# A transformer block on one core: rotations, masks, scalings and blanking of slots moved between VectorE, ScalarE and GpSimd, loads issued earlier, two layer norms folded into one

## The reference, cut to what matters

```python
# layer 0 attention: no weights; rotary turn of q = norm(x) and k = ctx, causal, 16 heads of 8
q, k = rope(heads(norm(x))), rope(heads(ctx)); out = softmax(mask(q k^T / sqrt(8))) v,  v = heads(ctx)
# layer 0 "ffn": a graph of 6 nodes, each an attention of 8 heads of 16 on weighted edges
q = ew[c,0]*(nodes[a] @ We + be); k, v likewise; nodes[c] = act_w[c]*(mha(q,k,v) @ Wo) + q
out = norm(nodes[5], 1e-6)*ln_g + ln_b
# layer 1 attention: its input is normed once by the block and once by the layer
xn = norm(norm(x))*gamma + beta; q = xn @ w_q; k, v = split(ctx @ w_kv); 16 heads of 64
# layer 1 ffn: 8-bit fake quantisation.  layer 2 attention: q = norm(x), k = v = ctx, causal and padded
# layer 2 ffn: quantised.  layer 3 attention: four projections.  layer 3 ffn: top-2 of 32 experts
```

## Time and profile before

| | us |
|---|---|
| median of 3 runs | 1889.33 (1886.15 to 1894.91) |
| the profiled execution's own time | 1894.12 |
| its span | 1892.3 |
| PE busy | 1303.1 (69%) |
| DVE busy | 1224.2 (65%) |
| ACT busy | 836.7 (44%) |
| POOL busy | 476.5 (25%) |

### The profile page before, as it was taken

The page is one execution under the profiler, slowest core; times in us unless marked ns, Lnnn a source line. Parts: engine busy times, 40 slices in busy tenths (PEclk is TensorE's granted clock), DMA queues, the critical chain, the costliest instruction groups (busy, mean ns, idle before and its releaser), DMA issues. The chain is left out here.

```text
span 1892.3 us, 32152 instructions
## 1 busy us (share of the span) xinstructions
PE 1303.1 (69%) x12243; PEld 922.7 (49%) x12245; DVE 1224.2 (65%) x2458; ACT 836.7 (44%) x1294; POOL 476.5 (25%) x650
## 2 busy tenths in 40 slices
PE   0798179999999991499899882179833688530674
PEld 0465056666666660366666650146622455320674
DVE  5665337777777777666776756836657577558444
ACT  1255226676776771355555532225513156410330
POOL 6343232222222201222222222134310200000452
PEclk9999579999999996599999996579965789965787
DMA  2243312222222222000000000122101122143434
GB/s 72 51 65 43 99 59 85 86 88 86 91 85 86 90 65 68 1 1 1 1 1 1 1 1 11 28 52 54 37 12 32 35 52 53 46 153 87 158 123 124
DMA packets 115782, 108.20 MB, mean 57 GB/s; under 512 B 44766, under 2 KB 99230, under 8 KB 114590
## 3 DMA queue, kind: packets, MB, share of 16 engines
q1 hardware_dynamic: 113582, 103.49, 19.8%
q0 software_dynamic: 2048, 2.65, 0.6%
HBM read 44.00 MB, written 8.71 MB: 28 GB/s over the span
## 5 line engine op out<-in xcount | busy, mean ns | idle before, releaser
L595 ACT ACTIVATE Pt<-bank 128x1024 f32<-128x1024 f32 (+1 forms) x384 | 366.4, 954 | 176.3 <-PE bank L539 174.7
L651 DVE TENSOR_REDUCE l0f_Mf<-bank 128x4 f32<-128x1024 f32 x192 | 234.5, 1221 | 108.8 <-PE bank L518 108.8
L559 PE MATMUL bank<-Pt,V 128*32 128x256 f32 (+1 forms) x3072 | 196.9, 375 | 10.7 <-POOL Pt L400 9.5
L1127 POOL TENSOR_TENSOR Psum<-Pt 128x512 f32<-128x512 f32 x64 | 83.5, 1305 | 269.8 <-ACT Pt L1259 269.8
L400 POOL TENSOR_SCALAR_AFFINE_SELECT Pt<-Pt 128x512 f32<-128x512 f32 x128 | 81.9, 640 | 176.1 <-ACT Pt L595 176.1
L559 PEld LDWEIGHTS bank<-Pt,V 128*32 128x32 f32 x3072 | 81.5, 111 | 82.3 <-issue 26.2
L416 POOL CAST parts<-nodes 128x256 fp32r<-128x256 f32 x96 | 38.4, 400 | 306.5 <-PE bank L490 306.5
L539 PE MATMUL bank<-l0f_QK 64*128 64x256 f32 x768 | 97.6, 333 | 19.4 <-DMA l0f_QK<-l0f_NMrow 18.9
L841 PE MATMUL bank<-ident,Qf 128*128 128x128 f32 x64 | 14.4, 418 | 140.2 <-SPq L243 91.6
L1297 DVE TENSOR_TENSOR qk_lo<-bank,qk_hi 128x512 fp32r<-128x512 f32 x64 | 44.2, 690 | 99.3 <-ACT qk_hi L1251 99.3
L651 DVE TENSOR_REDUCE l2x_Mf<-bank 128x4 f32<-128x1024 f32 x64 | 76.9, 1221 | 32.3 <-PE bank L518 32.2
(11 more groups left out here) (397 smaller groups left out, 3363.0 us busy)
## 6 DMA issues: line engine op xcount, KB each, us to landing
l0f_QK<-l0f_Z SPq DMA_DIRECT2D x288, 128.0 KB, 2.3
l2x_QK<-l2x_Z SPq DMA_DIRECT2D x96, 128.0 KB
V<-in_L_experts SPq DMA_DIRECT2D x8, 960.0 KB
Wg<-in_L_experts SPq DMA_DIRECT2D x8, 960.0 KB, 12.1
l0x_QK<-l0x_Z SPq DMA_DIRECT2D x48, 128.0 KB
tokB<-s_cand SPq DMA_DIRECT2D x16, 200.0 KB
s_y_even<-in_c_zero SPq DMA_DIRECT2D x1, 2048.0 KB, 11.2
s_y_odd<-in_c_zero SPq DMA_DIRECT2D x1, 2048.0 KB, 16.1
```

What stands on the lines that cost most here:

```text
L559: last = pe.matmul(bank[4][32 * x:32 * x + 32, o + q0:o + S], Va[:, 2 * n + k, 4 * j + x, :], Pp[:, (f + x // 2) % 4, x % 2, k * S:k * S + ...
L595: act.activation(Pp[:, g % 4, :, 0:w], banks[:, 2:4, 0:w], ACT.Exp, scale=L.scale).then_inc(exp_done, 1)
L651: d.tensor_reduce(m, A.rearrange("p h (t k) -> p h t k", t=2), AX, ALU.max).then_inc(max_done, 1)
L1127: e.tensor_tensor(Psum[:, q % 2], Pp[:, q % 4, :, 0:S], Pp[:, q % 4, :, S:2 * S], ALU.add).then_inc(key_sum, 1)
```

## The change

1. The loads of the first attention (`tA`, `ctxS`, `rope`, `rowk`) go to the head of `setup_sp`; `X` goes behind the barrier into `l0x_sp`. `setup_sp` then awaits nine loads. `rowk` is loaded once and its three later loads are gone. POOL clears `V` and writes the ones before the first barrier.
2. The rotation of `ctx` goes from POOL to DVE, in two halves, each put behind a request for a mean to PE.
3. Both halves of all slots are written by ACT (`slots_blank`), part of them before the root of the norm, part behind it: 6 of 128x2048, in the graph 8 of 128x1024. `queries_blank` and `keys_blank` are gone.
4. The graph's 12 scalings of weights go from POOL to DVE. After the graph the gate is multiplied in with `ln_g`, and POOL, behind its part of the flow, adds the gated `ln_b` to `X`; DVE has one instruction less over the whole of `X`.
5. Layer 1's loads (`l1x_in_sp`) and high parts (`l1x_in_act`) are issued before the barrier `l0f_end`. Its two norms become one, with the variance times 1.00001 plus 1e-10. POOL makes three low parts before the next barrier and the others, in pieces, behind it; PE waits for the pieces by `w_lo`. `Esel` is made from an 8-column sum and one copy.
6. Before layer 2 the values' copy goes from POOL to ACT and the mask to DVE.
7. Three semaphores of the expert part (`m_token`, `xg_out`, and the count) are replaced by `dma_out`.

The diff, without the plain renamings:

```diff
         y_full, y_done = sem("y_full"), sem("y_done")
         wd_in, w_full, w_hi, w_done = sem("wd_in"), sem("w_full"), sem("w_hi"), sem("w_done")
 
-        def queries_blank(g, L):
-
-            for r in range(L.ring):
-                g.eng.tensor_copy(L.QK[:, r, :, 0, :], bc(L.rowk[:, 0:1].unsqueeze(1), [P, L.blocks, S]))
-
-        def keys_blank(a, L):
-
-            for r in range(L.ring):
-                a.eng.copy(L.QK[:, r, :, 1, :], bc(L.rowk[:, 1:2].unsqueeze(1), [P, L.blocks, S]))
+        def slots_blank(a, L, which):
+
+            for k in which:
+                r, x = k // 2, k % 2
+                a.eng.copy(L.QK[:, r, :, x, :], bc(rowk[:, x:x + 1].unsqueeze(1), [P, L.blocks, S]))
 
         def values_ones(g, L):
...
         x_rows = T["x"].rearrange("b (t p) c -> p (b t) c", p=P)
-        N_IN = 6
+        N_IN = 9
 
         def setup_sp(s):
             e = s.eng
-            e.dma_start(X[:], x_rows).then_inc(dma_in, 16)
+            e.dma_start(tA[:], T["x_heads"]).then_inc(dma_in, 16)
+            e.dma_start(ctxS[:], T["ctx_heads"]).then_inc(dma_in, 16)
+            e.dma_start(rope[:], T["c_rope"]).then_inc(dma_in, 16)
+            e.dma_start(rowk[:], T["c_rows"]).then_inc(dma_in, 16)
             e.dma_start(ident[:], T["c_ident"]).then_inc(dma_in, 16)
             e.dma_start(cmaskf[:], T["c_mask"].rearrange("a p k -> p a k")).then_inc(dma_in, 16)
...
             s.barrier()
 
         def setup_pool(g):
+            g.eng.memset(ones[:], 1.0)
+            g.link(g.eng.memset(V[:], 0.0))
+            values_ones(g, L0)
             loaded(g, N_IN)
-            g.link(g.eng.memset(ones[:], 1.0))
             g.barrier()
...
             s.barrier()
 
         def l0x_pool(g):
-            g.link(g.eng.memset(V[:], 0.0))
-            values_ones(g, L0)
-            loaded(g, 4)
-            queries_blank(g, L0)
+            g.count("in", 1)
             g.link(g.eng.tensor_copy(v_view(L0)[:, :, :, 0:8], ctxS[:].rearrange("p t (h d) -> p t h d", d=8)))
-            rotate(g, ctxS[:], Kf[:], tB[:])
             g.barrier()
             flow_pool(g, L0, bases[0])
...
         def l0x_dve(v):
             d = v.eng
-            loaded(v, 4)
+            v.count("in", 1)
             xs = tA[:].rearrange("p t (h d) -> p (t h) d", d=8)
             xc = tC[:].rearrange("p t (h d) -> p (t h) d", d=8)
             sq = O[:].rearrange("p t (h d) -> p (t h) d", d=8)
             sh = [P, 256, 8]
             d.tensor_reduce(st1[:], xs, AX, ALU.add).then_inc(mean_ask, 1)
+            rotate(v, ctxS[:], Kf[:], tB[:], (0,))
             d.wait_ge(mean_full, 1)
             v.link(d.tensor_tensor(xc, xs, bc(bank[0][:, 0:256].unsqueeze(2), sh), ALU.subtract))
             v.link(d.tensor_tensor(sq, xc, xc, ALU.mult))
             d.tensor_reduce(st1[:], sq, AX, ALU.add).then_inc(mean_ask, 1)
...
             p.barrier()
 
         def l0x_act(a):
-            loaded(a, 4)
-            keys_blank(a, L0)
-            a.count("in", 1)
+            a.count("in", 2)
+            slots_blank(a, L0, range(6))
             rstd_act(a, 256)
             a.barrier()
...
         def l0f_pool(g):
             e = g.eng
             values_ones(g, L0f)
-            loaded(g, 17)
-            queries_blank(g, L0f)
-            for c in range(6):
-                e.tensor_tensor(WeS[:, c], WeS[:, c], bc(ew[:, 3 * c:3 * c + 1], [P, D]), ALU.mult)
-                g.link(e.tensor_tensor(Wn[:, 3, c], Wn[:, 3, c], bc(actw[:, c:c + 1], [P, D]), ALU.mult))
+            loaded(g, 16)
             g.barrier()
             g.barrier()
             flow_pool(g, L0f, bases[1])
+            g.link(e.tensor_tensor(lng[:, 1], lng[:, 1], bc(gates[:, 4:5], [P, D]), ALU.mult))
+            g.link(e.tensor_tensor(X[:], X[:], bc(lng[:, 1].unsqueeze(1), [P, NT, D]), ALU.add))
             g.barrier()
             g.barrier()
 
         def l0f_pe(p):
-            loaded(p, 17)
+            loaded(p, 16)
             p.barrier()
             transposes_pe(p, lambda t: Qf[:, t, :])
...
             p.barrier()
 
         def l0f_act(a):
+            slots_blank(a, L0f, range(4))
             rstd_act(a, NT)
-            loaded(a, 17)
-            keys_blank(a, L0f)
+            a.count("in", 16)
+            slots_blank(a, L0f, range(4, 8))
             a.barrier()
             empty(a, "A", put_plain(a, "A", nodes[:, 0]))
...
         def l0f_dve(v):
             d = v.eng
             ln_dve(v, X, Qf, 1e-5)
-            loaded(v, 17)
+            loaded(v, 16)
             for c in range(6):
                 e_ = NODES[c][0][0]
+                d.tensor_scalar(WeS[:, c], WeS[:, c], ew[:, 3 * c:3 * c + 1], None, ALU.mult)
+                d.tensor_scalar(Wn[:, 3, c], Wn[:, 3, c], actw[:, c:c + 1], None, ALU.mult)
                 d.tensor_tensor(ewbe[:, c:c + 1], ew[:, 3 * c:3 * c + 1], beT[:, e_:e_ + 1], ALU.mult)
             v.barrier()
...
             v.barrier()
             ln_dve(v, Qf, Qf, 1e-6)
             sh_ = [P, NT, D]
-            v.link(d.tensor_tensor(Qf[:], Qf[:], bc(lng[:, 0].unsqueeze(1), sh_), ALU.mult))
-            v.link(d.tensor_tensor(Qf[:], Qf[:], bc(lng[:, 1].unsqueeze(1), sh_), ALU.add))
-            v.link(d.scalar_tensor_tensor(out=X[:], in0=Qf[:], scalar=gates[:, 4:5], in1=X[:],
-                                          op0=ALU.mult, op1=ALU.add))
+            v.link(d.scalar_tensor_tensor(out=Qf[:], in0=Qf[:], scalar=gates[:, 4:5],
+                                          in1=bc(lng[:, 0].unsqueeze(1), sh_), op0=ALU.mult, op1=ALU.mult))
+            v.link(d.tensor_tensor(X[:], Qf[:], X[:], ALU.add))
 
         def l0f_end(seat):
...
                              (brow[:], row_bc("L1_xattn_b_out", D)),
                              (g1[:], row_bc("L1_xattn_gate", 1)), (ctxF, T["ctxT"])):
                 e.dma_start(dst, src).then_inc(dma_in, 16)
+
+        def l1x_in_act(a):
+            act = a.eng
+            loaded(a, 8)
+            act.copy(wt_hi[:, 2048:3072], wF[:, 2048:3072]).then_inc(split_hi, 1)
+            for c in range(2):
+                act.copy(ctxH[:, 1024 * c:1024 * c + 1024], ctxF[:, 1024 * c:1024 * c + 1024]).then_inc(split_hi, 1)
+            for c in range(2):
+                act.copy(wt_hi[:, 1024 * c:1024 * c + 1024], wF[:, 1024 * c:1024 * c + 1024]).then_inc(split_hi, 1)
+
+        def l1x_sp(s):
             s.count("in", 8)
             s.barrier()
...
         def l1x_pool(g):
             e = g.eng
 
-            def eye(c):
-                return bc(ident[:, c:c + 8].unsqueeze(2), [P, 8, P])
-            g.link(e.tensor_tensor(Esel[:], eye(0), eye(8), ALU.add))
-            g.link(e.tensor_tensor(Esel[:], Esel[:], eye(64), ALU.add))
-            g.link(e.tensor_tensor(Esel[:], Esel[:], eye(72), ALU.add))
+            def low(dst, src, hi, o):
+                e.tensor_tensor(dst[:, o], src[:, o], hi[:, o].bitcast(F32), ALU.subtract).then_inc(w_lo, 1)
             g.link(e.memset(NM[:], 0.0))
-            loaded(g, 8)
-            for c in range(3):
-                o = slice(1024 * c, 1024 * c + 1024)
-                e.wait_ge(split_hi, c + 1)
-                g.link(e.tensor_tensor(wt_lo[:, o], wF[:, o], wt_hi[:, o].bitcast(F32), ALU.subtract))
-            for c in range(2):
-                o = slice(1024 * c, 1024 * c + 1024)
-                e.wait_ge(split_hi, c + 4)
-                g.link(e.tensor_tensor(ctxL[:, o], ctxF[:, o], ctxH[:, o].bitcast(F32), ALU.subtract))
+            e.wait_ge(split_hi, 2)
+            low(ctxL, ctxF, ctxH, slice(0, S))
+            for r in range(2):
+                low(wt_lo, wF, wt_hi, slice(2048 + 512 * r, 2560 + 512 * r))
+            g.count("in", 8)
             g.barrier()
+            e.wait_ge(split_hi, 5)
+            pick = Rden[:, 0, 0:8]
+            for k in range(8):
+                for x in range(2):
+                    low(wt_lo, wF, wt_hi, slice(1024 * x + k * P, 1024 * x + (k + 1) * P))
+                if k == 1:
+                    g.link(e.tensor_tensor(pick, ident[:, 0:8], ident[:, 8:16], ALU.add))
+                    g.link(e.tensor_tensor(pick, pick, ident[:, 64:72], ALU.add))
+                    g.link(e.tensor_tensor(pick, pick, ident[:, 72:80], ALU.add))
+                    e.tensor_copy(Esel[:], bc(pick.unsqueeze(2), [P, 8, P])).then_inc(w_lo, 1)
+            for b in range(1, B):
+                low(ctxL, ctxF, ctxH, slice(b * S, (b + 1) * S))
             for kind, u, j in order1():
                 if kind == "B":
...
                 b, r = u // 2, u % 2
                 if kind == "P":
                     pe.wait_ge(lo_done, 4 + g)
+                    if g < 8:
+                        pe.wait_ge(w_lo, 5 + 2 * g + (g > 1))
                     w = slice(((4 * r) + j) * P, ((4 * r) + j + 1) * P)
                     cols = slice(b * S, (b + 1) * S)
...
                         pe.wait_ge(vch_free, 2)
                     elif u >= 2:
                         pe.wait_ge(nm_free, u - 1)
```

(56 more changed lines are left out.)

22 lines of the change are left out of this document (9 added, 13 removed).

## The result

Median 1825.3 us against 1891.4, ratio 0.9655 (95% interval 0.9623 to 0.9687). The same two kernels timed together twice more gave 0.9677 (0.9645 to 0.9708; 1818.6 against 1881.4) and 0.9682 (0.9657 to 0.9707; 1833.0 against 1890.1). The profiled execution took 1825.38 us, its span is 1823.7. The forecast was 1832.

The account below looks back on a forecast made before the run. Stretches between flows, with PE nearly idle, last as long as the slowest of DVE, ACT, POOL and loads. Terms sum to 57.3 us: profiled 1894.12 gives 1836.8, median to expect 1832.0; range 1818 to 1850.

Parts of the forecast that it names:

- Start: Up to the first flow: earlier loads, both rotations on DVE, end 44.4 instead of 55.0 us: -10.6 (bounds -3.7 and -12).
- Before the graph: Stretch before the graph: slots on ACT, weight scalings on DVE, barrier 5.4 us earlier: -5.4 (bounds +2.8 and -6).
- After the graph and the norm: After the graph through layer 1's norm: earlier loads and casts, one norm; barrier at 747.5 instead of 772.2: -24.7 us.
- Behind the barrier: Layer 1 behind its norm: DVE's subtractions and addition slowed beside POOL's pieces: +1 us (bounds 0 and 6.5).
- Rival (b): Layer 1: contention takes back 5.5 us behind the barrier and 4.2 on the scalings; total 1842; chance 9%.
- Before layer 2: Stretch before layer 2: values' copy on ACT, mask on DVE, ACT last at 1224.4 instead of 1237.0: -12.7 (bounds -8.4 and -13).
- Before layer 3: Stretch before layer 3: norm's scalings 4.20 instead of 9.14 us, PE's transposes follow: -4.9 (bounds -3 and -5.5).
- Rival (a): POOL's stand of 7 us moves and lies bare at the graph's first split: +7.3, total 1839 us; chance 8%.
- Rival (e): Shorter rests leave the graph's flow at a granted clock of 0.84: 68 us on top, total 1900; chance 2%.
- (c): Start: the nine loads land 7.8 us later, not 0.9; total 1839; chance 5%.
- (d): Half of the sum is held by landings and barriers that no engine's line shows; total 1861 us; chance 4%.
- (f): The steps are hidden anyway and nothing comes; total 1889 us; chance 2%.

Follow-up runs that it names:

- experiment 1: The changed kernel with the context's 12 rotation steps back on POOL behind the copy into V, loads still ahead; median 1831.4 us, DVE's last rotation step at 45.3.
- experiment 7: The kernel before with only layer 1's two norms made one; stretch 26.5 us, 6.9 less, ratio 0.9955 (0.9924 to 0.9985).
- experiment 3: The changed kernel with layer 2's mask back on POOL behind the loads, no small instruction ahead; 20.0 us to the order copies instead of 16.9, median 1830.7.

## Why the prediction was right

- **Start, -10.6, measured -11.0.** Loads landed at 10.4, not 9.6; the small steps were 4 x 0.42, not 0.47, and POOL's copy cost nothing beside the reduction (2.29), where I had taken 1.0. The text let the moved rotations look like the heart of it; experiment 1 shows them at 1.4 of the 11, the earlier loads at 6.2, and POOL's relief by the slots and `V` at 3.5.
- **Before the graph, -5.4, measured -6.3.** The ends as written, 234 and 238.98, give 5.0; where the other 0.4 comes from is not said. Behind the landing DVE took 2.9 us, not 4.0: the 12 scalings and six columns are paced at 0.20 and 0.07, less than their listed 0.28 and 0.15.
- **After the graph and the norm, -24.7, measured -24.2.** ACT is last at the barrier, as said (DVE idles 1.1 ahead of it), so -1.3 and not -1.7. The recorded text splits most of it into 10.8 for contention and 10.2 for the second norm; these can't be had one by one: alone the one norm brings 6.9 (experiment 7).
- **Behind the barrier, +1, measured 0** (31.9 to 32.8 us from the transposes to the first exponential, before 31.8 to 32.8). The four subtractions went from 2.49 to 3.48 and the addition from 2.29 to 2.44, and this fits into DVE's idle time ahead of the first `qk_lo`, 5.52 us before and still 3.97 after. The term was sized at the rotation's ratio of 2; measured are 1.4 and 1.07. Rival (b) falls.
- **Before layer 2, -12.7, measured -12.7.** ACT is last, at 1178.6. That the landing, the mask and the stand would all lie bare on POOL was right for the kernel before alone: without the casts and the copy ahead of it the stand hides under the loads, and the mask on POOL costs 3.1 (experiment 3).
- **Before layer 3, -4.9, measured -5.0.** The 16 scalings are at 4.20 and the transposes follow them, as said.
- **Rival (a)** falls: in the changed kernel POOL has no bare stand; its first split of the graph comes 0.5 us behind the copy ahead of it. The Trainium skill (Advanced Engine Details and Errata, Mode Summary), read as in the prediction, would leave TENSOR_TENSOR untouched beside POOL. The runs disagree: 3.48 against 2.49, 3.01 against 2.29, 1.91 against 0.17.
- **Rival (e)** falls: the graph's flow was granted 0.98. The argument against it, that the clock follows PE's busy share from flow to flow, rests on two flows and doesn't hold inside one: in layer 0's flow the clock fell in one execution and not in another behind ten us with the same 8.66 us of PE work.
- **Rivals (c), (d) and (f)** fall with the table: the first loads landed 1.7 us later, and each stretch gave what it was priced at within 1 us.
- **What is over**, 66.1 by the medians and 68.6 by the spans against 57.3: 1.9 are in the terms above. The rest lies in flows that the change leaves alone. 3.1 are layer 2's fall of the clock in the first profile of before. From layer 3's transposes to the end the three profiles of the changed kernel took 402 to 419 us, so a gain there can't be told. In the two later comparisons the medians are 62.8 and 57.1 apart. In layer 0's flow, leaving out the execution with the fall at 66, 3 to 4.6 us remain (159.5 and 160.0 before, 156.5 and 155.4 after). Both profiles of before have a short fall there that these two lack (0.60 for 4 us at 168 in the first), by an estimate 4 x 0.4 = 1.6 us; the rest, and up to 2.6 in layer 2's, stay unexplained, and whether the change has a part in them is open. That the third comparison, 57.1, meets the sum of 57.3 is luck: its stretches gave 59 too.
